# ScalarE's exponentials in front of the squares in every slot of a graph attention layer

## The reference

```python
def _L0_gnn_ref(h, adj_mask, W, a):          # h: [16, 1024, 256], after a layernorm
    Wh = jnp.einsum('bnd,od->bno', h, W)
    a1, a2 = (a[:256], a[256:])
    e = (Wh @ a1)[:, :, None] + (Wh @ a2)[:, None, :]
    e = jnp.where(e > 0, e, 0.2 * e)
    e = jnp.where(adj_mask == 0, -jnp.inf, e)
    alpha = jax.nn.softmax(e, axis=-1)
    return jnp.einsum('bij,bjo->bio', alpha, Wh)

x = x + _L0_gnn_ref(_layernorm(x), adj, W, a)
x = x + _L0_ffn_ref(_layernorm(x), ...)
```

## Time and profile before

| | us |
|---|---|
| median of 3 runs | 2808.19 (2808.19 to 2808.91) |
| the profiled execution | 2809.31 |
| its span in the trace | 2807.4 |
| attention part within it | up to about 684 |

### The profile page before, as it was taken

One profiled execution on the slowest core, in us unless ns is written; L12 is line 12 of the kernel. 1 busy time (PEld: TensorE's weight loads), 2 busy tenths in 40 slices (PEclk: granted clock), 3 DMA queues, 4 the chain that ended last, 5 costly groups with the idle time before them and its releaser, 6 DMA issues.

```text
span 2807.4 us, 46140 instructions
## 1 busy us (share of the span) xinstructions
PE 2774.5 (99%) x17114; PEld 2469.6 (88%) x17114; DVE 2413.1 (86%) x3408; ACT 2106.8 (75%) x2832; POOL 487.5 (17%) x707
## 2 busy tenths in 40 slices
PE   8999999999999999999999999999999999999998
PEld 7999999998788888888888888888888888888887
DVE  8999999997888888888888888888888888888887
ACT  7889889887777777777777777777777777777775
POOL 4555555555000000000000000000000000001000
PEclk9999999999999999999999999999999999999999
DMA  4455555543455554545445455545545554545554
GB/s 163 154 167 163 157 166 162 162 153 119 139 170 165 161 166 154 165 156 161 163 155 165 154 165 161 165 153 170 157 163 157 160 164 154 166 154 163 153 162 145
DMA packets 160060, 445.91 MB, mean 159 GB/s; under 512 B 16032, under 2 KB 73800, under 8 KB 159840
## 3 DMA queue, kind: packets, MB, share of 16 engines
q1 hardware_dynamic: 159840, 442.98, 50.2%
HBM read 401.99 MB, written 40.93 MB: 158 GB/s over the span
## 4 chain that ended last, share of the span: by engine, by line
PE 74%; DVE 1%; ACT 0%; issue 0%; DMA 0%; DVEq 0%; ACTq 0%
PE head_ps L53 12%; PE head_ps L55 12%; PE head_ps L54 12%; PE m_ps L1284 7%; PE m_ps L1287 7%; PE m_ps L1286 7%; PE z_ps L55 4%; PE z_ps L53 4%; PE z_ps L54 4%; PE turn_ps L1257 1%; PE turn_ps L1265 1%; DVE h_lo L1569 0%; DVE h_sums L1576 0%; DMA wo_ops<-wo_scratch 0%; ACT h_hi L1432 0%
## 5 line engine op out<-in xcount | busy, mean ns | idle before, releaser
L1416 ACT ACTIVATE h<-head_ps,bn_shift,bn_scale 128x512 f32<-128x512 f32 x768 | 593.9, 774 | 532.5 <-PE head_ps L55 319.9
L1569 DVE TENSOR_TENSOR h_lo<-h_sums,h_hi 128x1792 fp32r<-128x1792 f32 (+1 forms) x257 | 518.2, 2017 | 199.9 <-ACT h_hi L1432 199.8
L1432 ACT ACTIVATE h_hi<-h_sums 128x1792 fp32r<-128x1792 f32 (+1 forms) x257 | 435.4, 1694 | 63.6 <-DVE h_sums L1589 58.0
L1576 DVE TENSOR_TENSOR h_sums<-h,gate_row 128x1024 f32<-128x1024 f32 x256 | 313.7, 1225 | 114.5 <-ACT h L1416 96.7
L87 POOL TENSOR_TENSOR ffn_vareps<-ffn_mv,ln_eps 128x4 f32<-128x4 f32 x32 | 7.1, 223 | 1860.4 <-DVE ffn_mv L81 1860.4
L1536 DVE TENSOR_TENSOR h_lo<-h,h_hi 128x1024 fp32r<-128x1024 f32 x256 | 311.9, 1218 | 6.8 <-ACT h_hi L1446 6.8
L53 PE MATMUL attn_ps<-wh_hi,pT_hi 128*128 128x256 f32 x1024 | 304.9, 298 | 0.0
L54 PE MATMUL attn_ps<-wh_lo,pT_hi 128*128 128x256 f32 x1024 | 287.9, 281 | 0.0
L55 PE MATMUL attn_ps<-wh_hi,pT_lo 128*128 128x256 f32 x1024 | 287.8, 281 | 0.0
L1446 ACT ACTIVATE h_hi<-h 128x1024 fp32r<-128x1024 f32 x256 | 270.9, 1058 | 0.1
L1284 PE MATMUL m_ps<-h_hi,wo_ops 128*128 128x256 f32 x896 | 256.0, 286 | 3.1 <-DMA wo_ops<-wo_scratch 3.1
(11 more groups left out here) (215 smaller groups left out, 7619.3 us busy)
## 6 DMA issues: line engine op xcount, KB each, us to landing
wh_lo<-wo_scratch SPq DMA_DIRECT2D x124, 896.0 KB, 6.4
wo_ops<-wo_scratch SPq DMA_DIRECT2D x124, 896.0 KB, 6.5
adj_sb<-in_adj SPq DMA_DIRECT2D x128, 512.0 KB, 3.5
gate_row<-w_scratch SPq DMA_DIRECT2D x256, 256.0 KB, 4.6
x_sb<-in_x SPq DMA_DIRECT2D x64, 256.0 KB, 2.9
x_scratch<-x_sb SPq DMA_DIRECT2D x128, 128.0 KB, 1.8
ffn_x<-x_scratch SPq DMA_DIRECT2D x16, 512.0 KB, 7.6
x_sb<-x_scratch SPq DMA_DIRECT2D x16, 512.0 KB, 7.5
```

The source lines that it names most:

```text
L1416: return act.activation(dst, src, ACT.Relu, bias=bn_shift[layer][:, col], scale=bn_scale[layer][:, col])
L1432: act.activation(h2_hi[s % 2][:, a:b, :], g2[:, 1 + a:1 + b, :], ACT.Copy) \
L1569: dve.tensor_tensor(h2_lo[s % 2][:, a:b, :], g2[:, 1 + a:1 + b, :], bits(h2_hi[s % 2][:, a:b, :]), ALU.subtract).then_inc(S["h2_lo_ready"], 1)
L1576: dve.tensor_tensor(h2_rows, h2[:, :, :], gate[s % 2][:, :].unsqueeze(1).to_broadcast([P, KB, BANK]), ALU.mult).then_inc(S["gated_ready"], 1)
```

## The change

In most slots before, ScalarE did the negated mean and the squares first and the exponentials of another tile behind them. Only in the slot with u modulo 8 equal to 2, and in one slot at the end, the exponentials came first. Now they come first in every slot. The instructions are the same.

```diff
--- before.py
+++ after.py
@@ -829,9 +829,7 @@
                         act.wait_ge(first_tile.xT_psum, d + 1)
                         act.activation(first_tile.xT_hi[:, d, :], head_ps[:, d, :], ACT.Copy) \
                             .then_inc(first_tile.xT_hi_ready, 1)
-                exp_first = (head and head[1] == HEADS + 1) or (last and u == NORM_SLOT + 1)
-                if exp_first:
-                    exponentials(k, u, last)
+                exponentials(k, u, last)
 
                 post, pt, pn, pc = pair_at(k, u, 1, last)
                 if post:
@@ -849,8 +847,6 @@
                         act.wait_ge(S["x1_negmean_ready"], pn)
                         act.activation(w_sb[:, at % 2, :], x1_sb[at][:, :], ACT.Square, bias=x1_negmean[:, at:at + 1],
                                        accum_out=x1_squares[:, at:at + 1]).then_inc(S["x1_squares_ready"], 1)
-                if not exp_first:
-                    exponentials(k, u, last)
                 if u >= 0 and u % TASK_SLOTS == TASK_SLOTS // 2:
                     split_weights_hi(k, u // TASK_SLOTS)
                 if last and u == GATE_SLOT + 1:
```

## The result

The change made the kernel slower: 2820.41 us in the median of 5 runs (2819.67 to 2821.99) against 2808.19 (2806.75 to 2808.91) for the kernel before, a ratio of 1.0045 with a 95% interval of 1.003 to 1.0059. The profiled executions took 2819.67 and 2809.31 us, 10.4 apart. The prediction was 2815.3, in a range of 2808.5 to 2822.

What follows compares the result with a forecast made beforehand. In the attention part, a chain through VectorE (slots 2 to 7) and TensorE was taken to set the period. Steady 4.7, start 1.4 and last slots 1.0 sum to 7.1 us over the 2808.19 median: 2815.3, range 2808.5 to 2822.

Steps and rivals of the forecast that it cites:

- The mechanism: Attention part: earlier exponentials gain nothing; odd-slot squares 1.14 us later delay GpSimd's chain and, through denominators and collisions, VectorE.
- Steady part: Repeating 8-slot periods of the attention part: VectorE delayed in slots 2 and 4, +4.7 us in all, bounds 0 and 15.6.
- the two terms: Per steady period: late reciprocal after slot 2's masking, +0.16 us, and slot 4's masking waiting for GpSimd's add, +0.29.
- Start: First period: no slack for VectorE's reciprocal and a later scale; +1.4 us, bounds 0.5 and 2.5.
- the 1.1 of the text: First period: VectorE's reciprocal, already waiting for row denominators, comes 1.1 us later.
- the collision for which I gave 0.3: First period: a collision on the way to VectorE's scale that waits for GpSimd's rsqrt, 0.3 us more.
- Last slots: End of the attention part: reciprocal +1.2 us, then even-slot maskings meeting GpSimd's add; +1.0 us taken in all.
- the two cases: Last slots, add and masking starting within 0.05 us: masking first gives about -0.2 us in all, add first +2.3.
- the add comes first: Last slots: GpSimd's add wins over VectorE's masking, adding 0.4 us a pair of slots, to +2.3 in all.
- Rival A: TensorE's waits for exponentials are on every period's chain, so removing them gains about 11 us: 2797; chance 0.09.
- Rival B: Add hardly delays the masking; only row denominators' excess over their slack remains: 3 us slower, 2811; chance 0.18.
- Rival C: GpSimd's normalisations precede the waiting masking in slots 2 or 4, about 1.1 us each: 2829 or 2822; chance 0.06.

Runs made afterwards that it cites:

- e1: Kernel before, with exponentials in front of the squares in even slots only, old order in odd slots; 2809.14 us, ratio 0.9999.
- e2: Kernel before, with exponentials also in front of the squares in all odd slots, other even slots in the old order; 2819.88 us, ratio 1.0036.
- e4: Changed kernel, with GpSimd's row denominators one slot earlier, ahead of its wait for the squares; 2815.29 us, ratio 1.0025.
- e5: Changed kernel, with GpSimd's node-table add ahead of its wait for the squares (in the last pair only at its first odd slot); 2812.50 us, ratio 1.0013.
- e9: Changed kernel, with the old order in the last pair and in slots with u modulo 8 equal to 3; 2813.79 us, ratio 1.0017.
- e3: Changed kernel, with the slots of the last pair back in the old order; 2816.16 us, ratio 1.0026.
- e12: Kernel before, with the changed order in the last pair only; 2813.74 us, ratio 1.0014.
- e13: Changed kernel, with slot 11 of the last pair alone back in the old order; 2818.05 us, ratio 1.0030.

## Why the prediction was right, and where it was not

*The mechanism* held in its main line. Squares of odd slots alone make the loss (e1, e2), they do it through GpSimd's chain (e4, e5), and TensorE's time won at the exponentials is waited away at `wh_lo`: 8.3 us in 15 waits, 0.55 each, where 0.5 to 0.8 was forecast, and at `pT_lo`.

*Steady part:* forecast 4.7, measured 5.1; the period 41.1 as forecast. In the period shown above it is 2.62 us from the masking of slot 2 to the reciprocal and was 2.45, +0.17 for a forecast of 0.16, and 2.68 from the masking of slot 4 to its reciprocal for 2.41, +0.27 for 0.29. The masking of slot 4 took 1.47 to 1.52 us in 12 of 13 periods. But adding the two terms up as if each stood by itself was wrong, though the sum came out: take away the first (e4) and the collision grows by as much, so that nothing comes back; take away slot 3's delay (e9) and another collision takes its place.

*Start:* forecast 1.4, measured 1.5. The reciprocal waited 1.64 us against 0.57, the 1.1 of the text. The masking of slot 4 took 1.56 us against 1.21, the collision for which I gave 0.3, and the scale at `bn_rsqrt` then waited 0.25 as before. But the collision is not what costs there: in e2 and e3 that masking took 1.25 and 1.22 us, the scale waited 0.62 and 0.70 instead, and the period was as long (44.13 and 44.17). GpSimd's late chain sets the time by whichever of the two comes.

*Last slots:* this is the term that was mis-sized, 1.0 for a measured 3.7. The two starts did fall within 0.05 us of each other, as reckoned, and the two cases were priced rightly: the reciprocal gave +1.26 (its distance from the masking of slot 2 went from 2.72 to 3.98 us) and the three maskings +1.12 (7.06 for 5.94), together 2.4 where the text had 2.3 for "the add comes first". I took a value near the mean of the two cases, where each of the three collisions goes one way or the other (e12 got two of them the good way and one the bad). The rest, 1.3 us, was missing from the sum: in slot 11 the late square holds up `ffn_rstd`, which GpSimd computes behind the same chain, and through `ffn_xn` the first expert product (its wait went from 0.43 to 1.65 us; e13 takes it away). A search for everything queued on GpSimd behind the squares, not for the denominators alone, would have found it: VectorE already waited 0.32 us for `ffn_rstd` in the trace of before, and so there was no slack.

With 3.7 for 1.0, and 0.5 more from the other two terms, the 7.1 become 10.3, which is the difference of the profiled executions' spans. The medians differ by 12.2. The 5 runs of before beside after seem to have lain low: in the other comparisons before had 2808.57 to 2809.77, against which after is 10.6 to 11.8 longer, and e2, the same as after in the three stretches of the table, 10.7 longer than the before that ran with it.

*Rival A* (TensorE's waits count, 2797) fell with e1. *Rival B* (hardly anything, 2811) fell with the masking of slot 4, at 1.47 us and not 1.2. *Rival C* (GpSimd keeps the port, 2822 or more) had the near value and the wrong reason: no masking of the steady part took over 1.52 us, so the normalisations never went ahead of it.

## What to carry to other kernels

When a piece of work is moved back on one engine, list everything that stands behind its consumer in the consumer's queue, in the last iterations too, and compare each item's slack with the delay: here 1.14 us met slacks of 0.7, 1.0 and, at both ends of the loop, none. Waits of a busy engine are worth nothing to remove while another engine owns the loop; look for what it waits for next. Where two instructions that exclude each other would start at the same time, reckon with either outcome in full for each such meeting, and do not take the mean.

## What the runs showed of the hardware

- A masking that starts while GpSimd's add is under way is longer by nearly the whole overlap: the time over 1.20 us was the other's end less the masking's start less 0.11 to 0.13 in the collisions read here (0.27 of 0.38 at 314.00, 0.42 of 0.54 in e4, 1.15 of 1.28 at 643.60). The Trainium skill, page "SBUF — State Buffer", section "Who interferes with whom", says that the one that issued second waits for the other as a whole; the rows agree but for that tenth.
- With starts 0.01 us apart either engine can win. In e13 GpSimd's add took 2.37 us and the masking 1.22, in after the add 1.29 and the masking 2.35. One such tie makes 1.1 us in the masking; what VectorE kept of it was 0.85 (e12) and 0.86 (e13).
- A masking that already waits goes ahead of GpSimd's next instruction, tiny ones included: in after `row_den` took 1.18 us behind the add, and 0.19 when nothing competed.

```profile
644.84 1.18 POOL L555 TENSOR_TENSOR row_den<-row_sum,tiny 128x2 f32<-128x2 f32 x1
```

- The granted TensorE clock just ahead of the second half differed between executions of the same order there. The windows (stretch, length, busy us of PE with instructions, clock, DMA share, GB/s) of before, and of e2:

```profile
676.00:681.00 5.00, 4.57 (x16) 0.66 0.00 0
```

```profile
685.00:690.00 5.00, 4.51 (x11) 0.50 0.01 3
```

  At 0.50 it is the lower level. The last thing before the fall was TensorE's wait for `wh_hi`, 0.43 us in before and 1.65 in e2. But in e1 TensorE waited the same 0.42 us there and kept a clock of 1.00 up to 681 us; its first expert product took 0.50 us, and 0.80 in before. In e12 it waited the same 1.65 us as in e2 and kept 1.00 through the whole stretch. From the first expert product to the second half it took 5.3 to 5.5 us where the clock stayed high, 6.5 to 6.6 in before, after, e3, e4, e5 and e13, and 7.8 in e2. What decides it was not tested. Single executions of before spread over 2806.7 to 2812.6 us, and differences under some 2 us in a median are lost in that. This stretch, the start of the attention part (53.8 to 58.7 us to its first masking of a slot 2) and the second half (2123.7 to 2125.9 us) all vary between the traces by enough to account for it, but with one trace of before that is not shown.
